# Normalised branches scaled and added to the residual by one VectorE instruction a tile, with the shift carried in extra columns

## The reference

```python
x = x + ln(attention0(ln(x)))    # 16 heads of 16, rotary, causal softmax
x = x + ln(ffn0(ln(x)))          # silu(gate) * up, 768 hidden, integer weights
x = x + ln(attention1(ln(x)))    # 16 heads of 64, tanh soft clamp, causal
x = x + ln(ffn1(ln(x)))          # token shift, sigmoid(r) * (relu(k)^2 @ Wv)
```

## Time and profile before

| | |
|---|---|
| median of 3 runs | 1515.99 us (1515.74 to 1525.07) |
| profiled execution, its own time | 1519.53 us |
| span of the profiled execution | 1517.8 us |
| busy: PE, DVE, ACT, POOL | 1419.5, 1098.7, 800.0, 817.1 us (94, 72, 53, 54% of the span) |
| mean granted TensorE clock | 0.98 of full speed |
| DMA | 61.34 MB, mean 40 GB/s |

### The profile page before, as it was taken

The page is one execution under the profiler, slowest core; times in us unless marked ns, Lnnn a source line. Parts: engine busy times, 40 slices in busy tenths (PEclk is TensorE's granted clock), DMA queues, the critical chain, the costliest instruction groups (busy, mean ns, idle before and its releaser), DMA issues.

```text
span 1517.8 us, 32909 instructions
## 1 busy us (share of the span) xinstructions
PE 1419.5 (94%) x12438; PEld 1053.5 (69%) x12438; DVE 1098.7 (72%) x2040; ACT 800.0 (53%) x1135; POOL 817.1 (54%) x1002
## 2 busy tenths in 40 slices
PE   6889998998999898999999999999999999999997
PEld 4556766675767675777777777767667667677776
DVE  7888887788887867755648576576585665765766
ACT  2544444444443444555566665656566656566652
POOL 4344544454435352435667575675666565766652
PEclk8999999899999998999999999999999999999998
DMA  5221212102121213010100000010100100100001
GB/s 184 85 75 46 71 57 68 56 9 87 33 83 42 70 69 114 30 42 29 63 2 2 15 29 2 1 43 2 30 14 1 42 1 1 42 1 29 2 11 33
DMA packets 45763, 61.34 MB, mean 40 GB/s; under 512 B 3760, under 2 KB 31312, under 8 KB 45648
## 3 DMA queue, kind: packets, MB, share of 16 engines
q1 hardware_dynamic: 44784, 59.03, 11.4%
q10 hardware_dynamic: 864, 0.66, 0.2%
HBM read 25.83 MB, written 8.39 MB: 23 GB/s over the span
## 4 chain that ended last, share of the span: by engine, by line
PE 52%; POOL 16%; issue 14%; DVE 12%; DMA 3%; ACT 2%; SPq 1%; POOLq 0%; DVEq 0%; ACTq 0%
PE psum L442 25%; PE psum L1220 4%; PE psum L2102 4%; POOL l_keysum L1648 4%; POOL l_probs L321 4%; PE psum L2059 4%; PE psum L1190 3%; PE psum L1144 3%; POOL l_keysum L1650 3%; PE psum L2124 2%; PE psum L449 1%; POOL l_attT_lo L1661 1%; DVE l_rowmax L1005 1%; PE psum L1151 1%; POOL l_keysum L1652 1%
## 5 line engine op out<-in xcount | busy, mean ns | idle before, releaser
L1731 ACT ACTIVATE l_probs<-psum 128x1024 f32<-128x1024 f32 (+1 forms) x192 | 164.5, 879 | 170.6 <-PE psum L2059 133.0
L923 ACT ACTIVATE l_probs<-psum 128x512 f32<-128x512 f32 x256 | 138.3, 593 | 184.5 <-PE psum L1190 174.8
L321 POOL TENSOR_SCALAR_AFFINE_SELECT l_probs<-l_probs 128x256 f32<-128x256 f32 (+1 forms) x384 | 189.3, 524 | 0.0
L1005 DVE TENSOR_REDUCE l_rowmax<-psum 128x2 f32<-128x1024 f32 (+2 forms) x192 | 159.0, 862 | 27.8 <-PE psum L1151 27.1
L2102 PE MATMUL psum<-l_probs,l_v 128*32 128x512 f32 (+3 forms) x2048 | 154.2, 440 | 10.2 <-DVE l_qk_lo L1827 8.2
L1737 ACT ACTIVATE l_probs<-l_probs 128x2048 f32<-128x2048 f32 (+1 forms) x128 | 160.4, 1274 | 1.3
L1827 DVE TENSOR_TENSOR l_qk_lo<-psum,l_qk_hi 128x1024 fp32r<-128x1024 f32 x64 | 77.6, 1217 | 115.2 <-ACT l_qk_hi L1721 114.9
L1836 DVE RECIPROCAL l_keysum<-psum 128x256 f32<-128x256 f32 x64 | 112.2, 1754 | 47.2 <-PE psum L2088 40.6
L316 POOL TENSOR_TENSOR l_pool_holder<-expo 128x1 f32<-128x1 f32 x128 | 28.7, 224 | 200.7 <-ACT l_probs L1737 126.2
L2102 PEld LDWEIGHTS psum<-l_probs,l_v 128*32 128x32 f32 x2048 | 66.8, 111 | 92.4 <-issue 80.2
L1648 POOL TENSOR_TENSOR l_keysum<-l_probs 128x768 f32<-128x768 f32 x62 | 116.1, 1873 | 5.4 <-DVE l_att L1849 1.6
(11 more groups left out here) (239 smaller groups left out, 4196.5 us busy)
## 6 DMA issues: line engine op xcount, KB each, us to landing
l_kT<-l_roped_hi SPq DMA_DIRECT2D x32, 256.0 KB, 2.7
l_qT<-l_roped_hi SPq DMA_DIRECT2D x32, 256.0 KB, 2.5
l_xin<-in_x SPq DMA_DIRECT2D x8, 512.0 KB, 4.2
l_kT<-l_roped_lo SPq DMA_DIRECT2D x16, 256.0 KB, 2.8
l_qT<-l_roped_lo SPq DMA_DIRECT2D x16, 256.0 KB, 2.5
l_x<-in_x SPq DMA_DIRECT2D x8, 512.0 KB, 4.3
x_mid<-l_x SPq DMA_DIRECT2D x8, 512.0 KB, 3.0
l_xin<-x_mid SPq DMA_DIRECT2D x8, 512.0 KB, 4.6
```

Of the source, the lines that this page charges most:

```text
L321: nc.gpsimd.affine_select(out=part, in_=part, compare_op=ALU.is_ge, fill=0.0, base=0, pattern=[[0, part.shape[1]], [1, P]], channel_multip ...
L923: space.free(nc.scalar.activation(probs[:, SLOT[p], e, c0:c1], space.unit(*use), ACT.Exp, scale=HD0 ** -0.5), *use)
L1005: reduced = nc.vector.tensor_reduce(rowmax[:, a // 2, :, a % 2, t], space.unit("max", a, k)[:, :, c0:c0 + (t + 1) * P], mybir.AxisListType ...
L1731: space.free(nc.scalar.activation(probs[:, p % 2, :, c0:c1], space.unit("score", p, u)[:, :, 0:c1 - c0], ACT.Tanh, scale=HD1 ** -0.5 / CLA ...
```

## The change

The branch is no longer normalised and then added. One scalar_tensor_tensor a tile computes x += y * rstd, without the mean. The shift mean*rstd, one number a token, is kept beside the rows: `x1` gets 8 extra columns (two shifts of four tiles), `x3` gets 16. `x_mid` now holds for each batch and partition 1024 + 8 numbers in one piece, so its DRAM layout is [partition, 1032]. The final piece of the kernel, `x4_norm_tiles`, sums the four shifts of each token and subtracts the sum with the last branch. The addition on GpSimd (`x2`) is gone. Inner norms see rows that are off by the shifts.

```diff
+    def added(self, out, src, t):
+        return self.nc.vector.scalar_tensor_tensor(out=out, in0=src, scalar=self.rstd[:, t:t + 1], in1=out, op0=ALU.mult, op1=ALU.add)
+    def shift(self, out, tiles):
+        return self.nc.vector.tensor_tensor(out, self.mv[:, tiles, 0], self.rstd[:, tiles], ALU.mult)
...
         def o_norm(i):                                  # phase 1
             dve.wait_ge(norm_o.rstd_ready.sem, norm_o.rstd_ready.at(i, 1))
+            dve.wait_ge(res_loaded.sem, res_loaded.at(i, 16))
             for t in range(NT):
-                norm_o.apply(xn[:, t, :], xn[:, t, :], t).then_inc(o_normed.sem, 1)
-            dve.wait_ge(o_normed.sem, o_normed.at(i, NT))
-            dve.wait_ge(res_loaded.sem, res_loaded.at(i, 16))
-            nc.vector.tensor_tensor(x1[:], x1[:], xn[:], ALU.add).then_inc(x1_ready.sem, 1)
+                norm_o.added(x1[:, t, :], xn[:, t, :], t).then_inc(x1_ready.sem, 1)
+            norm_o.shift(shift[:, 0, :], slice(0, NT))
...
             for t in range(NT):                         # x2_norm
-                normed = norm_2.apply(x2n[:, t, :], half(t), t)
+                added = norm_2.added(x1[:, t, :], half(t), t)
                 if t % 2:
-                    space.free(normed, "down", t - 1)
-                else:
-                    normed.then_inc(x2_normed.sem, 1)
+                    space.free(added, "down", t - 1)
+            norm_2.shift(shift[:, 1, :], slice(0, NT)).then_inc(x2_ready.sem, 1)
...
-        def x2(i):                                      # GpSimd
-            pool.wait_ge(x2_normed.sem, x2_normed.at(i, NT // 2))
-            space.freed(pool, i, "down", 2)
-            nc.gpsimd.tensor_tensor(x1[:], x1[:], x2n, ALU.add).then_inc(x2_ready.sem, 1)
...
-            sp.dma_start(tok(x_mid, i), x1[:]).then_inc(x_stored.sem, 16)
+            sp.dma_start(x_mid[i], x1_raw[:]).then_inc(x_stored.sem, 16)
...
-            sp.dma_start(xin[:], tok(x_mid, i)).then_inc(x_loaded.sem, 16)
+            sp.dma_start(xin[:], rows_and_shifts(x_mid[i], 2)[0]).then_inc(x_loaded.sem, 16)
...
-            sp.dma_start(x3[:], tok(x_mid, i)).then_inc(res_loaded.sem, 16)
+            sp.dma_start(x3_raw[:, 0:NT * D + 2 * NT], x_mid[i]).then_inc(res_loaded.sem, 16)
...
+            dve.wait_ge(res_loaded.sem, res_loaded.at(i, 16))
             for t in range(tiles.start, tiles.stop):    # o_norm_tiles, phase 2
-                norm_o.apply(xn[:, t, :], o_half(t), t).then_inc(o_normed.sem, 1)
-            dve.wait_ge(res_loaded.sem, res_loaded.at(i, 16))
-            dve.wait_ge(o_normed.sem, o_normed.at(i, tiles.stop))
-            nc.vector.tensor_tensor(x3[:, tiles, :], x3[:, tiles, :], xn[:, tiles, :], ALU.add).then_inc(x3_ready.sem, 1)
+                norm_o.added(x3[:, t, :], o_half(t), t).then_inc(o_normed.sem, 1)
+            norm_o.shift(shift[:, 2, tiles], tiles).then_inc(shift_ready.sem, 1)
...
         def x4_norm_tiles(i, n, tiles):
             dve.wait_ge(norm_4.rstd_ready.sem, norm_4.rstd_ready.at(i, n))
+            norm_4.shift(shift[:, 3, tiles], tiles).then_inc(x4_shift.sem, 1)
+            dve.wait_ge(x4_shift.sem, x4_shift.at(i, n))
+            dve.wait_ge(shift_ready.sem, shift_ready.at(i, n))
+            nc.vector.tensor_reduce(shifted[:, tiles], shift.rearrange("p k t -> p t k")[:, tiles, :], mybir.AxisListType.X,
+                                    ALU.add).then_inc(shifted_ready.sem, 1)
+            dve.wait_ge(shifted_ready.sem, shifted_ready.at(i, n))
             for t in range(tiles.start, tiles.stop):
-                norm_4.apply(xn[:, t, :], xn[:, t, :], t).then_inc(x4_normed.sem, 1)
+                nc.vector.tensor_scalar(xn[:, t, :], xn[:, t, :], norm_4.rstd[:, t:t + 1], shifted[:, t:t + 1],
+                                        ALU.mult, ALU.subtract).then_inc(x4_normed.sem, 1)
             dve.wait_ge(x4_normed.sem, x4_normed.at(i, tiles.stop))
             nc.vector.tensor_tensor(x3[:, tiles, :], x3[:, tiles, :], xn[:, tiles, :], ALU.add).then_inc(x4_ready.sem, 1)
```

More of the change, by code:

```diff
@@ L325, in program @@
 def program(nc, a):
-    x_mid = nc.dram_tensor("x_mid", (BATCH, T, D), F32, kind="Internal").ap()
+    x_mid = nc.dram_tensor("x_mid", (BATCH, P, NT * D + 2 * NT), F32, kind="Internal").ap()
     tok = lambda ap, i: ap[i].rearrange("(t p) d -> p t d", p=P)
@@ L394, in split, with rows_and_shifts @@
             pe.wait_ge(self.low_done, count)
+def rows_and_shifts(raw, count):
+    rows = raw[:, 0:NT * D].rearrange("p (t d) -> p t d", d=D)
+    return rows, raw[:, NT * D:NT * D + count * NT].rearrange("p (k t) -> p k t", t=NT)
 class Norm:
@@ L514, in phase1 @@
     yT = [sbr("yT" + s, [P, NC, T], F32R) for s in ("_hi", "_lo")]
-    x1 = sbr("x1", [P, NT, D])
+    x1_raw = sbr("x1", [P, NT * D + 2 * NT])
+    x1, shift = rows_and_shifts(x1_raw, 2)
     gated = sbr("gated", [P, 2, T])
     hid = gated
-    yn = x2n = gated[:].rearrange("p a (t d) -> p (a t) d", d=D)
+    yn = gated[:].rearrange("p a (t d) -> p (a t) d", d=D)
     norm_o, norm_1, norm_2 = (Norm(nc, sbr, sig, expo, name, 1) for name in ("o", "x1", "x2"))
@@ L585, in phase1 @@
         "x2_norm": {(): 58.405},
-        "x2": {(): 57.687},
         "store": {(): 64.796},
@@ L710, in phase1 @@
     yT_hi = sig("yT_hi", 2 * NC)
-    x1_ready = sig("x1_ready", 1)
+    x1_ready = sig("x1_ready", NT)
     x2_ready = Signal(sem("x2_ready"), 1, before=1)
@@ L720, in phase1 @@
     rden_ready = sig("rden_ready", 4)
-    o_normed = sig("o_normed", NT)
-    x2_normed = sig("x2_normed", NT // 2)
     th_ready = sig("th_ready", NM)
@@ L808, in residual @@
                 sp.wait_ge(x_stored.sem, x_stored.at(i, 0))
-            sp.dma_start(x1[:], tok(a["x"], i)).then_inc(res_loaded.sem, 16)
+            sp.dma_start(x1, tok(a["x"], i)).then_inc(res_loaded.sem, 16)
         program(sp, {"fetch": lambda n: weights.load(sp, n), "place": place, "maxima": maxima, "load_x": load_x, "store": store,
@@ L838, in _ @@
                                 pattern=[[-1, P]], channel_multiplier=1).then_inc(consts, 1)
-        nc.gpsimd.memset(pool_holder[:, 0:1], 0.0).then_inc(x2_ready.sem, 1)
+        nc.gpsimd.memset(pool_holder[:, 0:1], 0.0)
         nc.gpsimd.memset(qT[:, 0:PAIRS // 2, :].bitcast(F32), 0.0).then_inc(q_cleared, 1)
@@ L876, in _ @@
             "o_rstd": lambda i: norm_o.gpsimd(pool, i, 0), "x1_rstd": lambda i: norm_1.gpsimd(pool, i, 0),
-            "hidden_lo": hidden_low, "x2_rstd": lambda i: norm_2.gpsimd(pool, i, 0), "x2": x2})
+            "hidden_lo": hidden_low, "x2_rstd": lambda i: norm_2.gpsimd(pool, i, 0)})
     @block.scalar
@@ L970, in _ @@
         nc.vector.memset(kT[:].bitcast(F32), 0.0).then_inc(k_cleared, 1)
+        nc.vector.memset(norm_2.holder[:], 0.0).then_inc(x2_ready.sem, 1)
         x_stats(0)
@@ L1348, in phase2 @@
     xn = sbr("xn", [P, NT, D])
-    x3 = sbr("x3", [P, NT, D])
+    x3_raw = sbr("x3", [P, NT * D + 4 * NT])
+    x3, shift = rows_and_shifts(x3_raw, 4)
     dx = sbr("dx", [P, NC, T])
@@ L1360, in phase2 @@
     mu = sbr("mu", [P, 2, NC])
+    shifted = sbr("shifted", [P, NT])
     norm_o, norm_3, norm_4 = (Norm(nc, sbr, sig, expo, name, 1) for name in ("o", "x3", "x4"))
@@ L1543, in phase2 @@
     yn_ready = sig("yn_ready", NT)
-    x3_ready = sig("x3_ready", 1)
+    shift_ready = sig("shift_ready", 1)
+    x4_shift = sig("x4_shift", 1)
+    shifted_ready = sig("shifted_ready", 1)
     x4_normed = sig("x4_normed", NT)
@@ L1884, in x3_stats @@
         def x3_stats(i):
-            dve.wait_ge(x3_ready.sem, x3_ready.at(i, 1))
+            dve.wait_ge(o_normed.sem, o_normed.at(i, HALVES[0].stop if last_batch(i) else NT))
             norm_3.statistics(dve, i, 0, lambda t: x3[:, t, :], EPS, 0 if last_batch(i) else None)
@@ L1889, in x3_stats_b @@
             if last_batch(i):
-                dve.wait_ge(x3_ready.sem, x3_ready.at(i, 2))
+                dve.wait_ge(o_normed.sem, o_normed.at(i, NT))
                 norm_3.statistics(dve, i, 0, lambda t: x3[:, t, :], EPS, 1)
```

3 lines of the change are left out of this document (1 added, 2 removed).

## The result

The changed kernel takes 1496.17 us (median of 6, 1490.64 to 1498.96); the kernel before, measured again beside it, 1517.07 us (median of 6, 1513.93 to 1525.07). The two medians are 20.9 us apart. The ratio is 0.9846, 95% interval 0.9823 to 0.9868: 1.5% or some 23 us less. The forecast was 10.7 us less. The direction was right, the size was half. The profiled execution of the changed kernel took 1490.64 us, its span is 1488.8 us; that of before had 1517.8. It is the fastest of the six, so the 29.0 us between the two profiled executions are more than the change gives in the middle.

A forecast was written before the change was run, and what follows sets the result against it. TensorE, busy 94% of the span, bounds the kernel; other engines count only where it stands. Terms -7.2 - 3.6 - 3.8 - 1.0 + 2.8 + 1.3 + 0.8 = -10.7 us take the median 1515.99 to 1505.3; range 1496 to 1520.

The forecast's parts named there:

- SP's queue, -7.2: Phase 1 loop: an earlier store lets q's low part go out 1.7 us sooner; 1.8 us less stand in four rounds.
- rival in which the low part was never held by the store: Phase 1 loop: the places' own issue time rules, stand and clock stay: 1514 to 1516 us; chance 0.17.
- The lowered clock, -3.6 in phase 1 and +1.3 in phase 2: TensorE's clock: two lowered phase 1 rounds recover, 1.3 and 2.3 us; phase 2's longer stand may lower it, +1.3.
- `o_norm` of phase 1, 0: Phase 1 attention branch: saves 1.0 us of VectorE per batch, off the path; additions still contend with GpSimd; no term.
- `o_norm` of phase 2, -3.8 and -1.0 outside: Phase 2 attention branch: GpSimd's masks back at 1.35 us, -0.95 in four rounds; one such gain outside the loop, -1.0.
- `x4_norm`, +2.8 and +0.8: Phase 2 last norm: shift costs one more apply-and-mask turn, 0.7 us in four rounds; 2 x 0.4 at the end.
- rival in which each tiny instruction loses a turn: Phase 2 `x4_norm`: both tiny instructions lose a GpSimd turn, clock falls: +3.6 us, 1520; chance 0.10.
- Layout, 0 +- 1: `x_mid` in DRAM: rows of 4128 bytes instead of 1024, total bytes unchanged, queues already dense: 0 +- 1 us.
- VectorE and GpSimd: Busy time over the whole kernel: 16 us less on VectorE, 19 less on GpSimd.
- good-end rival: Phase 1 stands vanish whole and every lowered clock in phase 2 goes too: -18, 1498 us; chance 0.17.

The follow-up runs named there:

- the reordered kernel: The kernel before with SP issuing the store of the rows behind the places of rope units 2 and 3: 1514.83 us against 1520.73, ratio 0.9968.

## Why the prediction was half of the gain

The median, 1496.17 us, is at the low edge of the forecast's range. By places the forecast had 10.8 us in the loop of phase 1, 1.0 outside the loops, 0.3 lost in the loop of phase 2 and 0.8 lost at the end. The two profiled executions show 14.7, 10.2, 4.8 gained and 0.8 lost. So most of what was missed lies outside the loops and in the clock of phase 2.

- **SP's queue, -7.2.** Right, in mechanism and nearly in size. The store did hold the low part of q, the stands went, and GpSimd's low part is the next condition. Undoing this part brings back 3.31, 1.71, 1.70 and 1.66 us, 7.3 us over the changed kernel's 1.07, of which 1.25 us a round is the net price where a later stand gives some back. The rival in which the low part was never held by the store has fallen: the reordered kernel removed the stand without touching GpSimd.
- **The lowered clock, -3.6 in phase 1 and +1.3 in phase 2.** This is the step that failed, and not by its price. A lowered round costs 1.3 us net beside the stand behind the masks, as the earlier trace rows had it, and filling the stands gave 3.4 us in three rounds of the profiled pair. What failed is how often it was counted. The forecast took the two lowered rounds of phase 1, nothing outside the loops, and a loss in phase 2. The trace of before has two lowered rounds in phase 2, where the forecast read one; they lost 2.1 and 1.9 us to the changed kernel, the two others 0.4 and 0.3. Its clock also fell near 110 and 186 us, at the seam and at the end of the program (12 products took 5.49 us, and 3.04 after), and the places near 110 and 186 alone gave 1.8 and 1.1 us. The longer stand behind `qk_lo` drew no lowered clock in the profiled execution of the changed kernel. In place of 2.3 us the clock gave 9 to 10 in the mean of all executions, by the line above. It was at hand before: the mean clock of 0.98 said that more was lost than two rounds. The forecast also let the clock stay up with under 1.97 us of standing left; in its own rows it fell behind 1.93, and in a later run behind 1.47.
- **`o_norm` of phase 1, 0.** Missed: a term put at nothing. The forecast took it for idle time of VectorE, and wrote that the new additions would still contend with GpSimd. They do, but GpSimd waits for instructions of 0.5 us and not for one of 1.2 to 1.4. TensorE stood behind the masks: 0.47 us a round and 0.65 near 110 us. The page "SBUF — State Buffer" of the Trainium skill says in "Who interferes with whom" that the loser waits for the whole instruction. The `hold` row agrees: it ends 0.05 us behind the addition beside it. So the length of one instruction was the number to ask for.
- **`o_norm` of phase 2, -3.8 and -1.0 outside.** The masks fell to 1.36 us, the stand by 0.9 to 1.0 us in each of four rounds: -3.8 as forecast. Outside the loop it was about 3 instead of 1.0; the stands of 0.61, 1.01 and 1.53 us at 810, 906 and 1492 us of the kernel before were not looked up.
- **`x4_norm`, +2.8 and +0.8.** Right in sign, measured +1.7 and +0.9. The shift does take the first gap, but then the applies run in 3.25 us instead of 4.91. The delay changed its victim and no turn was added. The rival in which each tiny instruction loses a turn is wrong: the sum over 16 numbers takes 0.18 us.
- **Layout, 0 +- 1.** Too small. The stands lost 1.5 us by it, and alone on the kernel before it gave 6.5 us (4 to 9). That the rest is clock is argued from the mean clock, not shown.
- **VectorE and GpSimd.** VectorE's busy time fell by 15.8 us (forecast 16). GpSimd's fell by 28.6 (forecast 19): 19.0 are the additions, 10 are masks that were blocked for less time. A scaled addition from PSUM takes 0.476 us (0.47), one from SBUF 0.544.

Standing alone, the forecast had -7.2 - 3.8 - 1.0 + 2.8 + 0.8 = -8.4 us and the profiled pair shows -12.3, after what the lowered clock had hidden of it in the kernel before. The good-end rival (1498 us, chance 0.17) came nearest, and only partly by its reasons. It had every lowered clock of phase 2 go, which came in the profiled execution. But it also had all stands of phase 1 vanish, where 1.07 us stayed, and it knew nothing of the masks and of the clock outside the loops; that its sum is within 2 us is in part luck.

## What to carry to other kernels

When TensorE is 94% busy, compare its busy time between equal rounds before summing its stands: a difference is clock. A stand that goes can take the lowered clock behind it with it. Count that in every stretch of the program and not in the loop that you study, and price it by the length of a round as well as by its busy time, because a later stand can take part of it up. Ask of each long VectorE instruction with two SBUF inputs which GpSimd instruction waits behind it, and split it if TensorE waits for that. When an order of a queue is changed, follow the wait to the next instruction of the same queue: the stand behind the store only moved to the residual, and it took an earlier store to remove it.
